# Zero writes on GpSimd behind every indirect gather of a two-layer graph network

## The reference

```python
# layer 0: messages from the source node's row, scaled by a sigmoid of the edge's 16 scalars
xs_e, xv_e = xs[src], xv[src]
...
messages = messages * jax.nn.sigmoid(edge_scalars @ W_rad.T + b_rad)
agg = jax.ops.segment_sum(messages, dst, num_segments=n)
...
x = _layernorm(x + _L0_gnn_ref(x, ...), axis=-1)
# layer 1: weights w from a small net on the 16 scalars, messages averaged over a node's edges
e0, e1 = f0[edge_src], f1[edge_src]
...
x = _layernorm(x + _L1_gnn_ref(x, ...), axis=-1)
```

## Time and profile before

| | |
|---|---|
| median of 3 runs | 4594.62 us (4580.94 to 4601.47) |
| the profiled execution's own time | 4584.39 us |
| its span | 4582.6 us |
| POOL busy | 3160.4 us (69%) |
| DVE busy | 4081.5 us (89%) |
| PE busy | 3690.7 us (81%) |
| ACT busy | 3390.5 us (74%) |
| granted TensorE clock, mean | 0.763 |

### The profile page before, as it was taken

One profiled execution on the slowest core, in us unless ns is written; L12 is line 12 of the kernel. 1 busy time (PEld: TensorE's weight loads), 2 busy tenths in 40 slices (PEclk: granted clock), 3 DMA queues, 4 the chain that ended last, 5 costly groups with the idle time before them and its releaser, 6 DMA issues.

```text
span 4582.6 us, 82591 instructions
## 1 busy us (share of the span) xinstructions
PE 3690.7 (81%) x16478; PEld 2488.1 (54%) x16479; DVE 4081.5 (89%) x12731; ACT 3390.5 (74%) x10840; POOL 3160.4 (69%) x3275
## 2 busy tenths in 40 slices
PE   5777777777777777777788999989999999999996
PEld 3555555665656655565564444444444444544446
DVE  4999999999999999999947899989899989888995
ACT  3777777777777777777657777777777777777873
POOL 3677777777777777777527777777777777777770
PEclk8555555555555555555589999999999999999998
DMA  8666666666666666666523333333333333333331
GB/s 263 176 181 182 179 180 179 181 182 178 181 179 182 179 182 181 179 183 179 149 68 103 102 103 103 103 102 103 102 102 103 102 102 103 102 103 102 103 100 37
DMA packets 325663, 642.03 MB, mean 140 GB/s; under 512 B 143598, under 2 KB 175147, under 8 KB 325531
## 3 DMA queue, kind: packets, MB, share of 16 engines
q0 software_dynamic: 181616, 557.94, 44.7%
q1 hardware_dynamic: 144016, 83.72, 6.7%
HBM read 620.52 MB, written 20.88 MB: 140 GB/s over the span
## 4 chain that ended last, share of the span: by engine, by line
DVE 50%; issue 18%; PE 12%; POOL 8%; DVEq 6%; ACT 4%; DMA 1%; SPq 0%; POOLq 0%; ACTq 0%
DVE total L573 16%; DVE work L558 10%; DVE onehot L608 9%; PE ps L851 8%; POOL work L339 8%; DVE total L576 4%; ACT work L417 3%; DVEq L624 2%; DVE work L596 2%; DVEq L669 2%; DVE dstf L652 2%; DVE work L603 1%; DVE acc L616 1%; DVE arena L616 1%; DVE half L599 1%
## 5 line engine op out<-in xcount | busy, mean ns | idle before, releaser
L339 POOL DMA_INDIRECT arena<-table,srcs x1616 | 1552.0, 960 | 686.0 <-issue 476.3
L339 POOL DMA_INDIRECT work<-table,srcs x1616 | 1563.4, 967 | 493.8 <-issue 452.9
L417 ACT ACTIVATE work<-arena,dst_sh 128x96 f32<-128x96 f32 (+1 forms) x4848 | 1417.4, 378 | 559.0 <-DVE arena L580 541.9
L417 ACT ACTIVATE work<-work,dst_sh 128x96 f32<-128x96 f32 (+1 forms) x4848 | 1502.9, 396 | 329.7 <-issue 218.5
L851 PE MATMUL ps<-work,onehot 128*128 128x384 f32 x3616 | 1322.5, 513 | 170.4 <-DVE onehot L608 94.3
L851 PEld LDWEIGHTS ps<-work,onehot 128*128 128x128 f32 x3616 | 676.7, 196 | 739.7 <-issue 271.4
L851 PE MATMUL ps<-arena,onehot 128*128 128x161 f32 x3616 | 1061.0, 473 | 3.9 <-DVE arena L580 3.9
L827 PE MATMUL ps<-wrad,escal 17*128 17x160 f32 x3232 | 548.2, 485 | 636.3 <-DVE arena L580 635.5
L851 PEld LDWEIGHTS ps<-arena,onehot 128*128 128x128 f32 x3616 | 907.7, 315 | 130.1 <-issue 114.1
L608 DVE TENSOR_SCALAR onehot<-iota,dstf 128x128 f32 x3616 | 812.0, 303 | 18.0 <-DVE arena L616 9.9
L827 PEld LDWEIGHTS ps<-wrad,escal 17*128 17x128 f32 x3232 | 395.6, 302 | 788.2 <-issue 478.8
(11 more groups left out here) (123 smaller groups left out, 2155.8 us busy)
## 6 DMA issues: line engine op xcount, KB each, us to landing
escal<-in_escal SPq DMA_DIRECT2D x404, 98.0 KB
arena<-table,srcs POOLq DMA_INDIRECT x1616
work<-table,srcs POOLq DMA_INDIRECT x1616
table<-work SPq DMA_DIRECT2D x49, 224.0 KB, 3.1
dst_sh<-in_dst_sh SPq DMA_DIRECT2D x404, 20.0 KB, 2.6
table<-work SPq DMA_DIRECT2D x7, 784.0 KB, 4.1
acc<-in_xd SPq DMA_DIRECT2D x1, 3920.0 KB, 26.9
arena<-in_xd SPq DMA_DIRECT2D x7, 560.0 KB, 5.9
```

What stands on the lines that cost most here:

```text
L339: pool.indirect_dma_start(out=rows[:, j, t, :], out_offset=None, in_=table, in_offset=bass.IndirectOffsetOnAxis(ap=srcs[:, b, j, t:t + 1], ...
L417: last = nc.scalar.activation(u[:, t, to:to + c1 - c0], r[:, t, c0:c1], ACT.Copy, scale=dst_sh[:, j, at:at + 1].bitcast(f32))
```

## The change

A new scratch tensor `spacer` of 4 x 160 floats a partition. Behind each indirect DMA GpSimd writes 160 columns of zeros into it, and the last of a supertile's four writes raises the new semaphore s_space. Before the gathers of the next supertile GpSimd waits until that semaphore has counted all supertiles before it. Nothing reads the tensor.

```diff
+SPACE = 160
...
+        spacer = sb("spacer", [P, TPS, SPACE])
...
+        s_space = [sem(f"spacers_written{l}") for l in range(2)]
...
                     pool.indirect_dma_start(
                         out=rows[:, j, t, :], out_offset=None, in_=table,
                         in_offset=bass.IndirectOffsetOnAxis(ap=srcs[:, b, j, t:t + 1], axis=0)).then_inc(s_rows[l][j], 16)
+                    last = nc.gpsimd.memset(spacer[:, t, :], 0.0)
+                last.then_inc(s_space[l], 1)
 
             def gathers(l):
                 pool.wait_ge(s_src[l][0], 16)
                 for j in range(SLOTS):
+                    if j > 0:
+                        pool.wait_ge(s_space[l], j)
                     gather(l, j, 0)
...
                         pool.wait_ge(s_ev2[l], s + 1)
                         pool.sem_inc(s_pool, 1)
+                        pool.wait_ge(s_space[l], s + SLOTS)
+                        pool.sem_inc(s_pool, 1)
                         if j == 0:
                             pool.wait_ge(s_src[l][b], loads * 16)
                             pool.sem_inc(s_pool, 1)
...
             pool.wait_ge(s_done[0], 1)
+            pool.wait_ge(s_space[0], SUPS)
```

## The result

The changed kernel takes 5378.07 us (median of 4 runs, 5375.98 to 5398.88) where the kernel before takes 4595.67 us (4 runs, 4580.94 to 4601.47): a ratio of 1.174 [1.171, 1.177], 782 us more. The profiled execution took 5379.66 us by its own time, with a span of 5377.8 us (795.2 us more than before) and a mean granted clock of 0.737. The forecast was 5500 us with a range of 5020 to 5740: the mechanism was right, one term was too large.

What follows compares the result with a forecast made beforehand. POOL was taken to bound layer 1 and DVE layer 0, with POOL bounding both after the change; layer 0's 372 and layer 1's 534 us gave 906 on 4584.4, so 5490, or 5500 us against the median, range 5020 to 5740.

Steps and rivals of the forecast that it cites:

- POOL paces layer 1 and lies 0.39 us a supertile under DVE in layer 0: Edge layers before the change: POOL needs 5.09 us a supertile in layer 1; in layer 0, 5.06 of DVE's 5.45.
- The wait: At supertile borders: 0.18 memset, 0.06 report and 0.85 release make 1.09 us where 0.305 stood.
- the two outside releases of the earlier trace: Gathers released by DVE's L558 after 0.96 us and by an index load after 0.83; basis for the 0.85 us release.
- whether the 0.305 us gap swallows the memset: Between gathers inside a supertile: answered no, so the memset's 0.18 us adds to the gap, giving 0.485 us.
- The rival of hidden memsets: Memsets run inside the 0.305 us gap between gathers, only the border grows: about 5064 us; chance 18%.
- Start to start or reported length: Memset cost on POOL: 0.17 us for 160 columns by start spacing, 0.30 by reported length, which adds 388 us.
- Dearer memsets: Each POOL memset costs its reported 0.30 us instead of 0.18: 388 us more, 5890 us; chance 8%.
- the forecast's estimate from this rule: DVE's L558 and L608 may block POOL's memsets through the shared port: 0.03 us each, 90 us in all, 5590.
- PE's clock: PE falls to its lower clock in layer 1; at 0.62 the period is 7.3 us, +360 us, 5860; chance 6%.
- Not slower: Memset and gather run side by side on GpSimd, POOL's pace stays 5.09 us, time 4595; chance 4%.
- the rival's condition: At the border, memset plus release (0.24 + 0.85) must end before the gather's 0.95 plus 0.305 us do.
- The shorter way out of layer 0: Work behind layer 0's last gather shrinks from 22 to a guessed 16 us, POOL being less far ahead: -6 us.

Runs made afterwards that it cites:

- the kernels with two halves of the last two sets: Changed kernel with supertiles writing alternate scratch halves, wait one supertile later: 340 columns 5315.28 us (third set), 160 columns 4814.20 us (fourth set).

## Why the prediction was right, and where not

**POOL paces layer 1 and lies 0.39 us a supertile under DVE in layer 0: right.** The layers grew by 331 and 473 us, which is 0.35 us a supertile less in layer 0, and came out equally long, and the memsets alone cost layer 0 a third of what they cost layer 1.

**The wait: right, in size too.** A gap of 1.09 us was forecast and 1.09 measured; the two outside releases of the earlier trace rows, 0.96 and 0.83 us with two carriers and one, were the right rows for it, for POOL's signal to itself takes 0.97 and 0.79. That the price comes from the place of the signal was shown by sending it one gather sooner, which made the wait free. That carriers cost shows in the kernel with the wait moved ahead, and in the 0.27 us where there is none. Of the 0.79 us the signal's own way is thus the smaller part.

**The step that failed is the one that asks whether the 0.305 us gap swallows the memset.** I took the answer for yes or no, and 0.305 + 0.18 = 0.485 us for the gap inside a supertile. It measured 0.41 us in the median (0.44 on average, the pauses below included). The memset occupies POOL for what its reported length says, 0.25 us, and only 0.16 of the 0.305 us come behind it: the other 0.145 us run beside it. So a memset of 160 columns adds 0.105 us in the median instead of 0.18, and one of 16 adds nothing. Without the pauses the mean gap is 0.417 us, 0.068 less than forecast at 2424 places, -165 us; the pauses give back some 50, and the lengths of the gathers and the borders 6. Together that is -109 us, and 906 - 109 = 797 against the 795.2 measured.

The rival of hidden memsets was therefore true for 16 columns and not for 160, and its time, 5064 us, was 314 us under the result. My argument against it, that extra queue instructions don't lengthen the gap, shows only that part of the gap runs beside the queue; it says nothing of which part a memset can use.

**Start to start or reported length.** The Trainium skill, Perfetto Trace Analysis, GPSIMD Engine Instruction, tells the reader to time this engine by starts. The forecast did so with 0.17 us a memset, against 0.30 by its estimate of the reported length, and the measured total was 111 us under its sum where reported lengths would have put it 388 us over. But that 0.30 was itself too long, for the spacers report 0.246 us in the median; and start-to-start spacing among memsets is not what one costs ahead of a gather either, 0.105 us.

**Dearer memsets: wrong in size, but the disturbance is there.** The spacers are 245 ns at the least and 246 in the median, and 256 on average: 0.01 us of disturbance, the allowance that I had made, 32 us in all and not 388. The port rule of the Trainium skill, SBUF — State Buffer, Who interferes with whom, has a DVE copy, cast or tensor_scalar that uses both ports block GpSimd. The trace agrees with it in kind: of the 3232 memsets 451 took over 270 ns, 447 of these overlap L568 or L618 (both TENSOR_SCALAR) and the other 4 a CAST of DVE; the 1724 that overlap no such instruction took 265 ns at most.

```profile
4684.10 0.96 DVE L618 TENSOR_SCALAR onehot<-iota,dstf 128x128 f32 x4
4684.18 0.47 POOL L345 MEMSET spacer<- 128x160 f32 x1
```

That is 0.01 us a memset where the forecast's estimate from this rule was 0.03. **PE's clock: wrong.** It was granted 0.92 in layer 1, down from 0.97, and well over the 0.70 from which it would decide. **Not slower: wrong,** for a memset starts at its gather's end and not beside it, so memset and release begin only there. With the memset a gather earlier the rival's condition is met, and the wait is free.

**The rest.** The shorter way out of layer 0 was forecast as -6 us and is -6.2. The waits for indices went, as forecast. The gathers of layer 0 took 0.967 us on average instead of 0.960, 11 us in all, which the other gathers and the borders bring down to the 6 us above.

The range took in all of this. The one part of the close sum that nothing in the forecast had foreseen is the pauses, whose 50 us happened to offset some of the gap's 165. The range did not know of conditions in which the kernel before is 30% slower and the change a gain; nothing in the first profile points to them.

## What to carry to other kernels

An engine that the busy table puts last can be the bound: divide the spacing of its instructions by their length plus gap, and where the gap never varies, every instruction put there costs time. Put a signal that an engine needs back from itself one instruction earlier than its wait, or give it a second buffer: here the second buffer was worth 564 of 795 us, and the earlier signal closed the same gap at the borders. Look, too, at what stands between a wait and the instruction that needs it: 0.27 us without a carrier, ahead of the loop, and 0.79 with one, in the loop. And of a gap between two instructions ask how much of it still has to come behind a new one, for it is neither all free nor all lost.

## What was not expected of the hardware

**Stops of PE that come and go with the set of runs.** In two sets the kernel before took 5983 and 6063 us; its trace of the 5983 us set shows PE standing in mid-group, and other kernels of both sets show the same waits without a named releaser (1996 to 2468 us). In two others, one of them on the same chip as the 5983, it took 4582 and 4583. With POOL's gathers 1.57 us apart instead of 1.27 the stops are all but gone (5373 us), and kernels in between take times in between (5673 to 5934 us). Neither the cause of the stops nor whether it is the slower gathers that end them was found.

**A pause of POOL at a fixed count.** In the changed kernel the second gather of a supertile now and then starts late. POOL's timeline:

```profile
1055.76 0.95 POOL L342 DMA_INDIRECT arena<-table,srcs  x1 [0.79 <-POOL spacer L345]
1056.71 0.25 POOL L345 MEMSET spacer<- 128x160 f32 x1
1058.78 0.95 POOL L342 DMA_INDIRECT arena<-table,srcs  x1 [1.82 <-issue]
...
1222.11 1.06 POOL L342 DMA_INDIRECT arena<-table,srcs  x1 [1.82 <-issue]
```

It does so every 104 gathers exactly, 26 supertiles or 163 us, in both layers: 1.82 us where 0.16 are usual, some 30 times, 50 us in all. The kernel before has 8 such gaps of 1.95 to 2.12 us in layer 0, 208 gathers apart, at every second of the same places, and none in layer 1; the kernels with two halves of the last two sets have none. In the set with the stops the kernel before has 8 in layer 1 too. So the pauses come in layers where waits hold POOL again and again, and not where it runs gather behind gather. What they are, the runs don't show.

**Part of the gap between gathers can be used.** 0.145 of 0.305 us hide other work of POOL (0.30 us at 16 columns and at none).

**Memsets that take longer beside DVE's L568 and L618.** The 451 of them cost 25 us over two layers, too little to see in a table of busy times; single lengths beside single DVE instructions show them.
